# A conv_preact kernel streaming 96 tiles through ten slots: a new place for four of every six loads in SyncE's order

## The chip, the cores and the metric

The kernel runs on one core of one Trainium2 chip. The metric is the device time of one execution in microseconds (us), as the median of several executions. Engines are named as in the profile: PE (TensorE), ACT (ScalarE), DVE (VectorE), POOL (GpSimd), SP (SyncE). SP does no arithmetic here: it issues all transfers between the chip's memory (HBM) and SBUF, on one queue that is carried out by 16 DMA engines.

## The reference

The input is `x` of 16 images, 768 channels, 64 x 64 pixels, in float32, and `offset` of 48 x 2. The output is `x + displace(group_norm(x), offset)`:

```python
def _gn(v, G=32, eps=1e-5):               # 24 channels to a group
    g = v.reshape(B_, G, C_ // G, H_, W_)
    m = jnp.mean(g, axis=(2, 3, 4), keepdims=True)
    s = jnp.var(g, axis=(2, 3, 4), keepdims=True)
    return ((g - m) / jnp.sqrt(s + eps)).reshape(v.shape)
...
    # displace: 48 positions of 16 channels each
    off_px = offset * SCALE
    off_int = lax.stop_gradient(jnp.round(off_px))
    sub = off_px - off_int
...
    shifted = x[:, ch[:, None, None], iyc[:, :, None], ixc[:, None, :]]
    shifted = shifted * mask[None]        # zero where the source lies outside
...
    kern = jnp.exp(-(kx * kx + ky * ky) / (2.0 * SIGMA * SIGMA))
    kern = kern / kern.sum(axis=(1, 2), keepdims=True)
    out = lax.conv_general_dilated(shifted, kern_c[:, None, :, :], window_strides=(1, 1), padding='SAME', feature_group_count=C, ...)
```

So each channel is normalised with the mean and variance of its group, shifted by a whole number of pixels (0, 16, 32 or 48 in each direction, about), smoothed with a 3 x 3 kernel that is a product of a column and a row, and added to `x`.

## The kernel before

The array is cut into 96 tiles of 128 partitions (16 channels by 8 images) and 4096 pixels, which is 2 MB each. Three tiles that share whole groups make a unit, and there are 32 units. SBUF holds ten slots of one tile each, and tile `n` lives in slot `n % 10`: SP loads it there, DVE adds the smoothed part in place, and SP stores it from there. So a load of tile `m` waits until the store of tile `m - 10` has landed (`stored`), and a store of tile `n` waits until DVE has done tile `n` (`tile_done`, which also counts one step of the setup, hence the `+ 2`).

The work on a unit `u` runs across the engines like this:

- PE adds up all pixels of the unit's three tiles in `sums` (L277 in the profile, 8 matmuls a tile, two records each) and waits at each tile for its load (`loaded`). ACT squeezes the result (L440), PE spreads the means to the channels (L287 to L289), and ACT copies them (L445).
- ACT squares each tile around its mean (L455), PE adds the squares up in `variances` (L329 to L337), ACT makes the variance of it (L463), and POOL works out the column weights (L241 to L254).
- ACT copies the source window of each tile, less the mean, into `frame` (L396, L406). DVE makes two passes over it for the rows (L654, L659) and three for the columns, which add into the slot (L663, L666, L669). The first of the three waits for POOL's weights.

PE's order is fixed by hand: it does the sums of unit `u + 1` around the variances of unit `u`. For an odd `u` all three tiles of `u + 1` come ahead of `variances(u)`, for an even `u` two of them do. So the weights of an odd unit wait behind the load of the last tile of the next unit.

SP's order is fixed by hand too. Ten loads come first. Then the stores run in the order of the tiles, and a table with six entries says which loads stand behind each store. Six tiles (two units) are called a pair here. For a pair that begins at tile `b`, load `i` (0 to 5) is that of tile `b + 10 + i`, and it takes the slot of tile `b + i`. In the text a load is called L and a store S with its tile (L34, S24), which is not to be mixed up with a line (L196). An instruction on SP that waits holds up everything behind it on SP. All transfers are 2 MB and go through the same queue. SP's lines are L191 (load) and L196 (store).

Of the kernel before, what the change touches and what calls it, by code (L numbers as in the profile page):

```python
# [5 lines left out]
def build(nc, x, offset, out):  # L6
# [44 lines left out]
    def of_tile(tiles, n):  # L51
        block, half = ORDER[n // UT]
        return tiles[block * UT + n % UT, half]
# [9 lines left out]
    with ctx:  # L63
# [106 lines left out]
        def slot_px(n, a=0, b=PIX):  # L170
            s = n % SLOTS
            return xs[:, s * PIX + a:s * PIX + b]
# [11 lines left out]
        @block.sync  # L184
        def _(sp):
            sp.dma_start(given[:, :, :], offset.partition_broadcast(P)).then_inc(offset_loaded, 16)

            def load(n):
                if n >= SLOTS:
                    sp.wait_ge(stored[n % SLOTS], 16 * (n // SLOTS))  # L190
                sp.dma_start(slot_px(n), of_tile(x_tiles, n)).then_inc(loaded[n % SLOTS], 16)  # L191

            def store(n):

                sp.wait_ge(tile_done, n + 2)
                sp.dma_start(of_tile(out_tiles, n), slot_px(n)).then_inc(stored[n % SLOTS], 16)  # L196

            for n in range(SLOTS):
                load(n)

            AGAIN = [(), (0, 1), (), (2,), (3,), (4, 5)]
            for n in range(TILES):
                store(n)
                for i in AGAIN[n % len(AGAIN)]:
                    m = n - n % len(AGAIN) + i + SLOTS
                    if m < TILES:
                        load(m)
            for s in range(SLOTS):  # L210
                sp.wait_ge(stored[s], 16 * len(range(s, TILES, SLOTS)))
# [507 lines left out]
```

## Time and profile before

| | |
|---|---|
| median of 3 runs | 1015.58 us (1015.21 to 1016.88) |
| the profiled execution, its own time | 1013.46 us |
| its span in the profile | 1011.4 us |
| busy: DVE, PE, ACT, POOL | 82%, 79%, 65%, 39% |
| DMA traffic | 403.10 MB, mean 399 GB/s |
| granted TensorE clock, mean | 0.891 |

The span is the time between the first and the last instruction of the profile, and 2.1 us of the execution's own time lie outside it. Busy shares are means over the whole span. The granted clock is a share of 2.4 GHz.

### The profile page before, as it was taken

How to read it: one execution, taken by the hardware profiler on the slowest of the kernel's cores; microseconds unless marked ns; L12 is line 12 of the kernel's file. 1: busy time of each engine (PE TensorE's matmuls, PEld its weight loads, DVE VectorE, ACT ScalarE, POOL GpSimd, SP SyncE). 2: the span in 40 equal slices, each digit the busy share in tenths (PEclk: the TensorE clock that was granted, in tenths of full speed). 3: DMA queues.
4: the chain of work that ended last, by engine and by line, in shares of the span. 5: the costliest groups of instructions: out<-in, count | busy, mean ns of one | idle time of the engine just before them, and what ended most of it. 6: DMA issues, size and time to landing. Idle time of an engine off the chain costs nothing.

```text
span 1011.4 us, 9224 instructions
## 1 busy us (share of the span) xinstructions
PE 800.2 (79%) x2146; PEld 391.3 (39%) x2146; DVE 828.3 (82%) x550; ACT 657.8 (65%) x555; POOL 394.2 (39%) x348
## 2 busy tenths in 40 slices
PE   1999896988987889696997988888787898978710
PEld 0544343434533435343443533434243443434310
DVE  7588989979879895997969796877959879676796
ACT  7477756567776758576676763746755667783771
POOL 0404547356443401836343262503427336231302
PEclk9999997898889898797999899899898988889955
DMA  8987999999999999999999999999999999999967
GB/s 366 429 360 292 427 425 413 365 411 402 400 412 403 397 413 409 424 415 418 404 408 420 416 428 411 422 416 418 416 391 424 411 415 399 399 402 387 412 259 301
DMA packets 27822, 403.10 MB, mean 399 GB/s; under 512 B 3216, under 2 KB 3216, under 8 KB 3216
## 3 DMA queue, kind: packets, MB, share of 16 engines
q1 hardware_dynamic: 27792, 402.71, 97.0%
q8 instruction: 17, 0.28, 0.1%
q14 instruction: 13, 0.11, 0.0%
HBM read 201.38 MB, written 201.33 MB: 398 GB/s over the span
## 4 chain that ended last, share of the span: by engine, by line
DMA 44%; DVE 22%; PE 12%; ACT 7%; POOL 6%; issue 4%; ACTq 2%; DVEq 2%; SPq 1%; POOLq 0%
DMA out_dram<-xs 36%; PE sum_ps L277 10%; DMA xs<-x_dram 8%; DVE xs L663 5%; ACT frame L396 5%; DVE xs L666 5%; DVE smooth L659 4%; DVE xs L669 4%; DVE smooth L654 4%; POOL small L245 2%; POOL small L248 2%; POOL small L241 2%; ACT unused L455 1%; ACTq L374 1%; DVEq L658 1%
## 5 line engine op out<-in xcount | busy, mean ns | idle before, releaser
L277 PE MATMUL sum_ps<-xs,bands 128*128 128x512 f32 x992 | 499.3, 662 | 31.0 <-DMA xs<-x_dram 31.0
L455 ACT ACTIVATE unused<-xs,small 128x4096 bf16 (+1 forms) x94 | 348.7, 3709 | 16.7 <-ACT small L445 7.1
L396 ACT ACTIVATE frame<-xs,small (+1 forms) x96 | 223.3, 2326 | 176.9 <-DVE smooth L659 174.3
L277 PEld LDWEIGHTS sum_ps<-xs,bands 128*128 128x128 f32 x992 | 207.3, 214 | 285.9 <-issue 260.1
L241 POOL TENSOR_TENSOR small<-small 128x3 f32<-128x3 f32 x32 | 39.4, 1232 | 576.9 <-ACT small L463 576.9
L654 DVE SCALAR_TENSOR_TENSOR smooth<-frame,xs 128x1700 f32 (+5 forms) x96 | 163.5, 1703 | 91.3 <-ACT frame L406 71.7
L277 PE MATMUL sum_ps<-xs,halves 128*128 128x512 f32 x496 | 221.1, 599 | 20.9 <-DMA xs<-x_dram 20.9
L663 DVE SCALAR_TENSOR_TENSOR xs<-smooth,small,xs 128x1700 f32 (+5 forms) x96 | 163.6, 1704 | 60.8 <-POOL small L254 58.5
L659 DVE SCALAR_TENSOR_TENSOR smooth<-frame,xs,smooth 128x1700 f32<-128x1700 f32 (+5 forms) x96 | 163.6, 1704 | 10.4 <-DVE smooth L654 7.3
L669 DVE SCALAR_TENSOR_TENSOR xs<-smooth,small,xs 128x594 f32 (+9 forms) x96 | 159.7, 1664 | 3.4
L666 DVE SCALAR_TENSOR_TENSOR xs<-smooth,small,xs 128x594 f32 (+9 forms) x96 | 159.7, 1664 | 3.4
L277 PEld LDWEIGHTS sum_ps<-xs,halves 128*128 128x128 f32 x496 | 93.6, 191 | 144.8 <-issue 111.8
L248 POOL TENSOR_SCALAR small<-small 128x1 f32<-128x1 f32 x96 | 122.4, 1275 | 8.4
L254 POOL TENSOR_SCALAR small<-base_w,small 128x3 f32<-128x3 f32 x96 | 119.5, 1245 | 9.5
L245 POOL TENSOR_SCALAR small<-small 128x1 f32<-128x1 f32 x96 | 112.1, 1167 | 3.3
L287 PE MATMUL mean_ps<-small,halves 128*128 128x1 f32 x62 | 14.9, 309 | 91.7 <-ACT sum_ps L440 91.7
L463 ACT ACTIVATE small<-var_ps,small 128x3 f32<-128x3 f32 x32 | 8.2, 255 | 79.6 <-PE var_ps L337 77.2
L287 PEld LDWEIGHTS mean_ps<-small,halves 128*128 128x128 f32 x62 | 12.2, 247 | 106.2 <-ACT sum_ps L440 106.2
L406 ACT ACTIVATE frame<-small 128x64 f32 x96 | 31.4, 327 | 12.5 <-ACT frame L396 0.6
L445 ACT ACTIVATE small<-mean_ps 128x3 f32<-128x3 f32 x31 | 5.4, 175 | 38.2 <-PE mean_ps L289 38.2
L440 ACT ACTIVATE sum_ps<-sum_ps 128x512 f32<-128x512 f32 x31 | 19.1, 617 | 9.2 <-PE sum_ps L277 9.2
L329 PEld LDWEIGHTS var_ps<-small,bands 128*128 128x128 f32 x62 | 11.9, 194 | 18.8 <-issue 18.8
(128 smaller groups left out, 280.5 us busy)
## 6 DMA issues: line engine op xcount, KB each, us to landing
xs<-x_dram SPq DMA_DIRECT2D x96, 2048.0 KB, 11.0
out_dram<-xs SPq DMA_DIRECT2D x96, 2048.0 KB, 15.4
smooth<-offset_dram SPq DMA_DIRECT2D x1, 48.0 KB, 4.1
```

Source lines behind the costliest of these rows:

```text
L241: V.tensor_tensor(rstd0, var, power, ALU.pow).then_inc(rstd_step, 1)
L245: V.tensor_scalar(fix[:, column], var[:, column], rstd0[:, column], rstd0[:, column], ALU.mult, ALU.mult).then_inc(rstd_step, 1)
L248: V.tensor_scalar(rstd[:, column], fix[:, column], -0.5, 1.5, ALU.mult, ALU.add).then_inc(rstd_step, 1)
L254: V.tensor_scalar(col_w[:, now * UT + i, :], base_w[:, position, :], rstd0[:, column], rstd[:, column], ALU.mult, ALU.mult).then_inc(col_w ...
L277: last = nc.tensor.matmul(sum_ps[:, :], (FIRST, SAME, SECOND)[i], slot_px(n, c * BANK, (c + 1) * BANK), start=(i == 0 and c == 0), stop=(i ...
L396: nc.scalar.activation(frame[:, bass.ds(b, rows * PITCH)].rearrange("p (r c) -> p r c", c=PITCH)[:, :, LEFT:LEFT + W], xs[:, bass.ds(a, ro ...
L455: nc.scalar.activation(unused[:, :], xs[:, bass.ds(n % SLOTS * PIX, PIX)], ACT.Square, bias=neg_mean[:, i:i + 1], accum_out=squares[:, i:i ...
L654: V.scalar_tensor_tensor(sm, frame_window(-1), side_w[:, bass.ds(n, 1), 0], frame_window(0), ALU.mult, ALU.add).wait_op(tile_done, done_co ...
L659: V.scalar_tensor_tensor(sm, frame_window(1), side_w[:, bass.ds(n, 1), 1], sm, ALU.mult, ALU.add).wait_op(half_smooth, done_count, "sem-ge ...
L663: V.scalar_tensor_tensor(x_window(0, rows), sm, col_flat[:, bass.ds(weights + 1, 1)], x_window(0, rows), ALU.mult, ALU.add).wait_op(smooth ...
L666: V.scalar_tensor_tensor(x_window(1, rows), sm[:, 0:rows - 1], col_flat[:, bass.ds(weights, 1)], x_window(1, rows), ALU.mult, ALU.add).wai ...
L669: V.scalar_tensor_tensor(x_window(0, rows - 1), sm[:, 1:rows], col_flat[:, bass.ds(weights + 2, 1)], x_window(0, rows - 1), ALU.mult, ALU. ...
```

## The change

The table of loads behind stores is replaced. Nothing else differs, and the number of loads, stores and waits is the same.

```diff
-            AGAIN = [(), (0, 1), (), (2,), (3,), (4, 5)]
+            AGAIN = [(), (0,), (), (1,), (2,), (3, 4, 5)]
             for n in range(TILES):
                 store(n)
                 for i in AGAIN[n % len(AGAIN)]:
```

Load 0 stays behind the second store of the pair. Load 1 moves from there to behind the fourth store, load 2 from behind the fourth to behind the fifth, load 3 from behind the fifth to behind the sixth. Loads 4 and 5 stay behind the sixth store. In the last pair but one, load 1 (tile 95) is the last load of all.

On SP, before, a pair in the steady part of the program stands like this. The first row are loads 4 and 5 of the pair ahead, the last are loads 4 and 5 of this pair:

```order
L191 DMA xs<-x_dram 128x4096 x2
L196 DMA out_dram<-xs 128x4096 x2
L191 DMA xs<-x_dram 128x4096 x2
L196 DMA out_dram<-xs 128x4096 x2
L191 DMA xs<-x_dram 128x4096
L196 DMA out_dram<-xs 128x4096
L191 DMA xs<-x_dram 128x4096
L196 DMA out_dram<-xs 128x4096
L191 DMA xs<-x_dram 128x4096 x2
```

On SP, with the change, the same place of the program (the first row are loads 3, 4 and 5 of the pair ahead, the last those of this pair):

```order
L191 DMA xs<-x_dram 128x4096 x3
L196 DMA out_dram<-xs 128x4096 x2
L191 DMA xs<-x_dram 128x4096
L196 DMA out_dram<-xs 128x4096 x2
L191 DMA xs<-x_dram 128x4096
L196 DMA out_dram<-xs 128x4096
L191 DMA xs<-x_dram 128x4096
L196 DMA out_dram<-xs 128x4096
L191 DMA xs<-x_dram 128x4096 x3
```

Counted in transfers, load 1 moves from the fourth place of the pair's twelve to the sixth, load 2 from the seventh to the eighth, load 3 from the ninth to the tenth. Stores 2 to 5 each move one place ahead. Load 0, loads 4 and 5 and stores 0 and 1 keep their places. No other engine's order changes.

## Rows read from the trace of the kernel before

**Rows 1.** The page: the queue's share of the span, and the chain that ended last.

```profile
q1 hardware_dynamic: 27792, 402.71, 97.0%
DMA 44%; DVE 22%; PE 12%; ACT 7%; POOL 6%; issue 4%; ACTq 2%; DVEq 2%; SPq 1%; POOLq 0%
```

**Rows 2.** The chain in order of time, some DMA pieces: start us, us, what.

```profile
2.09 18.29 DMA xs<-x_dram
...
268.22 14.12 DMA out_dram<-xs
...
355.23 14.54 DMA xs<-x_dram
...
905.18 14.56 DMA xs<-x_dram
```

**Rows 3.** The timeline of SP: start us, us to the last issue's end, issues.

```profile
60.92 6.92 SPq L191 DMA_DIRECT2D xs<-x_dram  x2
82.13 3.62 SPq L196 DMA_DIRECT2D out_dram<-xs  x2
...
318.77 5.27 SPq L191 DMA_DIRECT2D xs<-x_dram  x2
324.08 0.96 SPq L196 DMA_DIRECT2D out_dram<-xs  x2
339.38 0.34 SPq L191 DMA_DIRECT2D xs<-x_dram  x1
339.76 0.45 SPq L196 DMA_DIRECT2D out_dram<-xs  x1
344.24 0.34 SPq L191 DMA_DIRECT2D xs<-x_dram  x1
...
476.56 10.05 SPq L191 DMA_DIRECT2D xs<-x_dram  x2
...
628.23 1.79 SPq L196 DMA_DIRECT2D out_dram<-xs  x2
...
905.18 10.06 SPq L191 DMA_DIRECT2D xs<-x_dram  x2
...
931.49 5.20 SPq L191 DMA_DIRECT2D xs<-x_dram  x2
```

**Rows 4.** L191, loads L34 and L35, then L36 and L37.

```profile
L191 SPq DMA_DIRECT2D xs<-x_dram x2: 340/340/340, 318.8 to 323.7; - x2
DMA to landing us min/median/max: 10.2/10.5/10.8
...
L191 SPq DMA_DIRECT2D xs<-x_dram x2: 340/340/340, 339.4 to 344.2; - x2
DMA to landing us min/median/max: 10.9/13.4/15.8
```

**Rows 5.** The timeline of PE from 581 us: start, us, what, [idle before, releaser].

```profile
581.23 7.11 PE L277 MATMUL sum_ps<-xs,bands 128*128 128x512 f32 x16
...
589.12 0.38 PE L287 MATMUL mean_ps<-small,halves 128*128 128x1 f32 x2 [0.78 <-ACT sum_ps L440]
...
593.09 8.59 PE L277 MATMUL sum_ps<-xs,bands 128*128 128x512 f32 x16 [3.14 <-DMA xs<-x_dram]
...
612.58 8.83 PE L277 MATMUL sum_ps<-xs,bands 128*128 128x512 f32 x16 [2.65 <-DMA xs<-x_dram]
```

**Rows 6.** Waits, first of 268.2 to 369.8 us, then of 629.7 to 795: us, times, longest.

```profile
PE sum_ps L277 <- DMA xs<-x_dram: 6.7, 4, 3.7
...
PE sum_ps L277 <- DMA xs<-x_dram: 19.8, 10, 3.4
```

**Rows 7.** The timeline of PE at the last unit's sums, same columns.

```profile
949.68 7.11 PE L277 MATMUL sum_ps<-xs,bands 128*128 128x512 f32 x16
967.89 0.59 PE L287 MATMUL mean_ps<-small,halves 128*128 128x1 f32 x2 [11.10 <-ACT sum_ps L440]
```

## The prediction

> **What bounds the kernel now.** I read the page first, then the chain of waits, then the order and landing of the transfers. The one queue's packets fill 97.0% of the time of 16 engines, so on the face of it the kernel is bound by transfers and a new order of the same transfers can give nothing. The chain says less: DMA is 44% of it, and DVE, PE, ACT and POOL hold 47% [rows 1]. In order of time the chain is on DMA in a few long stretches (the first from 268.22 us to the end of a piece at 355.23 + 14.54 = 369.8, the last ending at 905.18 + 14.56 = 919.7) and on computing between them [rows 2]. So the two take turns, and only what DMA saves in its own stretches can shorten the kernel.
>
> How long are these? 44% of 1011.4 is 445 us, less the first load's piece of 18.3 us [rows 1, 2], which the change can't touch: 427 us.
>
> **Busy is not full speed.** A load is issued the moment its slot's store has landed, so its time to landing tells how fast the queue moved. Where two transfers were ahead of it, three had to pass, and 14.54 and 14.56 us for three [rows 2] make 4.85 us for one. Where one transfer was ahead it should take 9.7 us. It takes more. L34 is issued at 318.77 with only S25 ahead: 10.2. L35 comes at 323.7 with only L34 ahead: 10.8, of which 0.5 is L34's own delay, so 0.6. L36, at 339.38 with S27 ahead, takes 10.9, so 1.2 over, and S28 is issued 0.38 us behind it. L37 has L36 and S28 ahead: 15.8, which is 14.55 and L36's 1.2, so it adds nothing [rows 3, 4]. The loads with two ahead that the chain shows add nothing either [rows 2]. For a whole pair: from 476.56 to 905.18 are seven pairs in 428.62 us, 61.2 each, where twelve transfers at 4.85 are 58.2 [rows 3]. The 3.0 us between are lost while the engines count as busy, and the four loads with one ahead (loads 0, 1, 2 and 5) are where I can see them go.
>
> **The change, part by part.** Nothing is added or removed on any engine. What changes is how much is in the queue when a load is issued. Walking through the new order with stores that are ready when their turn comes:
>
> - Load 0 is issued when store 0 lands, with store 1 alone ahead, as before. Stores 2 and 3 are now issued right behind it, so it looks more like L36 (1.2) than like L34 (0.5), whose successor came 4.9 us later. I take 0.8 and keep 0.5 and 1.2 as bounds.
> - Load 1 waits for store 1, which has long been ahead of load 0: load 0, stores 2 and 3 are in the queue, three ahead. Load 2 has three ahead (store 3, load 1, store 4), load 3 four, load 4 three, load 5 two (loads 3 and 4). By L37's row each of these is free.
>
> So the pair loses 0.8 us where it lost 3.0, and saves 2.2 (1.8 to 2.5). DMA-led stretches are 427 / 61.2 = 7.0 pairs: 15.4 us.
>
> Not all of that arrives. In the first stretch, 101.6 us long, PE idled for loads 6.7 us in four waits. From 629.7 to 795 it idled 19.8 us in ten [rows 6]. Per 100 us that is 6.6 against 12.0, so computing stands close behind DMA in the first stretch and takes over there sooner. Of its 101.6 / 61.2 x 2.2 = 3.7 us I count a third, which takes off 2.4. In the computing stretches I count nothing.
>
> **What the move costs.** Load 1 lands two transfers later, 9.7 us, and it is the last tile of a unit, for which PE waits. Take L59: PE began its sums at 581.23, and as L59's place lies right behind L58's, issued with one ahead 4.9 us after it, like L34 and L35, I place its landing near 578. The sums would start at 587.8 instead, 6.5 us later. Behind them, PE now idles 0.78 us for ACT, 3.14 for L60 and 2.65 for L62 [rows 5], and L60 and L61 come one transfer later too. PE would be through with L61 at about 614.5 and begin L62, which keeps its place in the queue, some 2 us behind the present 612.58. It has taken 8.6 to 8.8 us over a tile after such an idle time and 7.1 in a row of work [rows 5], so it ends L62's sums about where it does now. Behind these are the weights of tile 57 and S57. S57 is issued at about 628.23 + 1.79 - 0.34 = 629.7 [rows 3]. Its new turn comes five transfers after L62's landing (near 612.5), at 636.8, so 7 us of cover are left before the queue runs dry, where 12 were. I cost this at nothing. If the cover is gone, S57 and load 1 of that pair, now behind it on SP, are late by what exceeds it.
>
> At the start, L11 was issued at 60.92 + 6.92 - 0.34 = 67.5, and then SP had nothing to issue until S2 at 82.13. Now L11 stands behind S3, which comes at 82.13 + 3.62 - 0.33 = 85.4 [rows 3], 18 us later. Computing is the bound there until 268 us, and the later loads meet PE with some backlog, so I cost it at nothing, and at up to 2 us as a bound. At the end, L95 is issued behind S87 instead of S85, 9.7 us later than at its present 936.3. PE began its sums at 949.68, and then waited 11.10 us for ACT [rows 7]. L95's landing would move to about 957 less what was saved by then, and the sums would end by 964 even without it, ahead of 967.9. Nothing.
>
> **Sum.** 15.4 - 2.4 = 13.0 us faster. The profiled execution took 1013.46 us of its own, so 1000.5. The median of the runs lies 2.1 above it: 1002.5.
>
> **The rivals.**
>
> A: computing takes over almost at once. DVE is busy 82% of the span, and each stretch of the chain hands over to it. Then each DMA stretch gives perhaps half a microsecond a pair before DVE, ACT and PE are the bound: 3 to 6 us faster, 1011. For it: load 1's lateness falls on PE just when it has least to do, and in the first stretch PE idles little. Against it: PE idles for loads about 12 us in 100 from 629.7 on [rows 6], which is 7 in a pair, three times what the pair would save.
>
> B, slower: the excess doesn't come from the depth of the queue, and stays. Then nothing is saved and only the lateness is left. L59's case shows the price: PE 2 us late on L62, and where it isn't made up by faster matmuls, up to 0.5 us of it reaches each of seven pairs after the cover: 3.5 us slower, 1019. It decides once a pair saves less than 0.5 us. Against it: L36 and L37 are 5 us apart, both with a store ahead, and only the one with one transfer ahead is slow [rows 4].
>
> The Trainium skill speaks for B: DMA: Bandwidth & Descriptors, Anatomy of one DMA, gives a transfer a fixed part of about 2 us besides its bytes at 436 GB/s, and its rules for kernel authors say that this part overlaps when a transfer is issued early. One transfer of 4.8 us ahead would cover 2 us, so a second ahead would buy nothing, and the 3.0 us a pair would be something else, with the time of B. The trace disagrees as far as it goes, with 10.2 to 10.9 us for loads with one ahead where 9.7 would do.
>
> C: more arrives, all of 2.5 us a pair, the first stretch too, and computing stretches shorten as PE finds its tiles loaded: 17 us or more, 998 or below. Against it: DVE and PE have 18 and 21% of the span idle, so far more than that would have to come out of their own chain.
>
> D: no change, where A's small gain meets B's lateness.
>
> **How the numbers follow.** My forecast (8 to 17 us faster) has 0.60, A 0.14, C 0.10, D 0.05 and B 0.11. The range runs from 993 (C with its whole 3.0 us a pair, and 2 us from computing stretches) to 1012.5 (A's lower end), and leaves out B, D and little of C. The likeliest case's own range is 998.5 to 1007.5. A measurement of this kernel can tell about 0.2%, 2 us, from no change. Faster by more holds the forecast, A's most part and C: 0.83. Same: 0.06. Slower: 0.11.
>
> **What the profile after should show.** A pair in DMA-led stretches near 59 us where it was 61.2. Loads 1 to 5 issued with two or more ahead, with landing times of 14.5 us and up in whole multiples of 4.85, and load 0 alone at 10.2 to 10.9. DMA's share of the chain falls, that of DVE and PE grows. Store 3 of each pair (S57 is one) is issued at DVE's pace, with the queue nearly empty at times in computing stretches. I am wrong if loads with three ahead still lose a microsecond, if load 1's lateness shows as PE idle before the last sums of even pairs and then in DVE's wait for weights, or if the granted clock falls as PE idles less.

## The result and the profile after

The changed kernel takes 1010.85 us (median of 20 runs) against 1016.74 us (20 runs of the kernel before, the three shown above among them). The ratio is 0.9948, with a 95% interval of 0.993 to 0.9965: 0.5% faster, some 5 us, where 13 us were forecast. The direction was right and 1010.85 lies in the stated range of 993 to 1012.5, but the size of the gain was not right. The profiled execution has a span of 1008.2 us, where it was 1011.4.

The page of the changed kernel: the queue's line, and the chain that ended last. Behind it stands the same last line of the kernel before.

```profile
q1 hardware_dynamic: 27792, 402.71, 96.2%
DMA 30%; PE 23%; DVE 23%; ACT 8%; POOL 6%; issue 5%; ACTq 2%; DVEq 2%; SPq 0%; POOLq 0%
DMA xs<-x_dram 27%; PE sum_ps L276 20%; DVE xs L662 5%; DVE xs L665 5%; ACT frame L395 5%; DVE smooth L658 5%; DVE xs L668 4%; DVE smooth L653 4%; DMA out_dram<-xs 4%; POOL small L240 2%; POOL small L244 2%; POOL small L247 1%; ACTq L373 1%; ACT unused L454 1%; DVEq L657 1%
```

```profile
DMA out_dram<-xs 36%; PE sum_ps L277 10%; DMA xs<-x_dram 8%; DVE xs L663 5%; ACT frame L396 5%; DVE xs L666 5%; DVE smooth L659 4%; DVE xs L669 4%; DVE smooth L654 4%; POOL small L245 2%; POOL small L248 2%; POOL small L241 2%; ACT unused L455 1%; ACTq L374 1%; DVEq L658 1%
```

Against [rows 1], DMA's share of the chain has fallen from 44 to 30%, and PE's has grown from 12 to 23%. All line numbers behind the table are smaller by one. Most of what DMA gave up, PE has taken, and the lines by name say where: before, stores held 36% of the chain and loads 8%. Now loads hold 27%, stores 4%, and PE's sums 20% where they held 10%. The chain runs through loads and the PE that waits for them.

The timeline of SP in the changed kernel (start us, us to the last issue's end, issues), one pair in the second half and the place that the prediction counted from and to:

```profile
473.58 10.05 SPq L191 DMA_DIRECT2D xs<-x_dram  x2
...
623.02 0.34 SPq L191 DMA_DIRECT2D xs<-x_dram  x1
623.41 7.62 SPq L196 DMA_DIRECT2D out_dram<-xs  x2
631.07 0.98 SPq L191 DMA_DIRECT2D xs<-x_dram  x1
637.69 0.33 SPq L196 DMA_DIRECT2D out_dram<-xs  x1
639.06 0.34 SPq L191 DMA_DIRECT2D xs<-x_dram  x1
...
894.74 10.05 SPq L191 DMA_DIRECT2D xs<-x_dram  x2
```

The same seven pairs as in [rows 3] take 894.74 - 473.58 = 421.16 us, 60.2 each. It was 61.2, and 59 were forecast. In the pair shown, S56 and S57 are issued 7 us apart (623.41, and 623.41 + 7.62 - 0.34 = 630.7), since S57 waits for DVE, and L65 (load 1) comes right behind.

The landing of three groups of loads in the changed kernel, load 0 (L64), loads 1 and 2 (L65, L66) and loads 3 to 5:

```profile
L191 SPq DMA_DIRECT2D xs<-x_dram x1: 340/340/340, 623.0 to 623.0; - x1
DMA to landing us min/median/max: 11.1/11.1/11.1
...
L191 SPq DMA_DIRECT2D xs<-x_dram x2: 340/662/985, 631.1 to 639.1; - x2
DMA to landing us min/median/max: 17.6/18.5/19.4
...
L191 SPq DMA_DIRECT2D xs<-x_dram x3: 328/340/340, 643.9 to 663.4; - x3
DMA to landing us min/median/max: 14.6/19.4/24.3
```

Loads 2 to 5 behave as forecast: 14.6 is three transfers, 19.4 four, 24.3 five, nothing over. Load 0, with one ahead, takes 11.1 where 9.7 would do, so it loses 1.4 us here, more than the 0.8 that was taken and than the upper bound of 1.2. This pair is kind to load 1. Over all pairs (what each landing in the trace comes later than 4.85 us behind the one before it) load 0 loses 1.2 us on average and load 1 0.6: between 1.0 and 1.8 in each of the first seven pairs, nothing in the last eight. In the kernel before, loads 0, 1, 2 and 5 lost 0.2, 0.8, 0.9 and 1.1.

The waits of the whole span, first in the kernel before, then in the changed one (us, times, longest):

```profile
DVE smooth L654 <- ACT frame L406: 71.7, 37, 5.1
...
PE sum_ps L277 <- DMA xs<-x_dram: 51.9, 26, 3.7
...
ACT sum_ps L440 <- PE sum_ps L277: 9.2, 1, 9.2
```

```profile
PE sum_ps L276 <- DMA xs<-x_dram: 102.4, 34, 6.9
DVE smooth L653 <- ACT frame L405: 91.5, 43, 7.4
...
ACT sum_ps L439 <- PE sum_ps L276: 50.4, 12, 9.2
```

PE idles 102.4 us for loads, where it was 51.9. Tile by tile, 72.3 us of it are for load 1, for which PE never idled before, and 24.3 for load 3. ACT waits for PE's sums 50.4 us in 12 waits, where it was one wait at the start. DVE waits 20 us more for ACT's frame. Take L29. In the kernel before, this is PE at its sums and at the means behind them (start, us, what, [idle before, releaser]):

```profile
277.86 7.11 PE L277 MATMUL sum_ps<-xs,bands 128*128 128x512 f32 x16
289.45 0.59 PE L287 MATMUL mean_ps<-small,halves 128*128 128x1 f32 x2 [4.48 <-ACT sum_ps L440]
```

and in the changed kernel

```profile
284.99 9.29 PE L276 MATMUL sum_ps<-xs,bands 128*128 128x512 f32 x16 [6.00 <-DMA xs<-x_dram]
295.06 0.38 PE L286 MATMUL mean_ps<-small,halves 128*128 128x1 f32 x2 [0.78 <-ACT sum_ps L439]
```

Before, PE didn't wait for L29 and idled 4.48 us ahead of the means, 3.7 more than the 0.78 that remain now. Now it idles 6.00 us for L29, runs the sums at 9.29 us instead of 7.11, and the means come 5.6 us later. The landing of L29, first in the kernel before, then in the changed one:

```profile
L191 SPq DMA_DIRECT2D xs<-x_dram x1: 340/340/340, 261.9 to 261.9; - x1
DMA to landing us min/median/max: 10.7/10.7/10.7
```

```profile
L191 SPq DMA_DIRECT2D xs<-x_dram x1: 1970/1970/1970, 270.2 to 270.2; - x1
DMA to landing us min/median/max: 14.7/14.7/14.7
```

It landed at 261.9 + 10.7 = 272.6 and now does at 270.2 + 14.7 = 284.9, 12.3 us later and not 9.7. Its store (S21) does wait for DVE, but the queue didn't run dry there: S20 was under way until 273.6. The trace shows the other 2.6 us as L28, ahead of it, landing 1.7 us later than before, and L29 losing 0.9 us more in the queue than it did. And DVE is late in turn. ACT squeezes the sums between the frames of tiles 25 and 26, so its wait of 4.2 us for PE puts off the frame of tile 26. DVE's first pass over it, before and after, with DVE's wait for the frame:

```profile
303.54 3.55 DVE L654 SCALAR_TENSOR_TENSOR smooth<-frame,xs 128x3200 f32 x1 [1.36 <-ACT frame L406]
```

```profile
308.52 3.55 DVE L653 SCALAR_TENSOR_TENSOR smooth<-frame,xs 128x3200 f32 x1 [5.04 <-ACT frame L405]
```

The last pass of tile 27 on DVE, before and after:

```profile
324.07 0.54 DVE L669 SCALAR_TENSOR_TENSOR xs<-smooth,small,xs 128x306 f32 x1
```

```profile
329.06 0.54 DVE L668 SCALAR_TENSOR_TENSOR xs<-smooth,small,xs 128x306 f32 x1
```

So by tile 27 DVE is 5.0 us behind the kernel before. Of these, 3.7 are this wait. The rest it had from the start: it was 0.3 us behind at tile 8 and 1.5 at tile 11, whose own load (L11) landed 22.8 us later than before.

The issues and landings of all 192 transfers show where the span goes. With no loss and no gap, each of the 191 behind the first would land 4.85 us after the one before it, 926.4 us in all. The first landing and the end take 11 to 12 us. What comes on top, in us:

| | before | changed | loads 2 and 3 moved alone (e2 below) |
|---|---|---|---|
| lost with transfers in the queue | 53.3 | 41.0 | 31.3 |
| queue empty, and starting again | 20.5 | 29.5 | 26.3 |
| span | 1011.4 | 1008.2 | 996.1 |

The change took 12.3 us of loss out of the queue and put 9.0 us of emptiness in.

### The profile page after: what moved, and what is told of

Its sections match the earlier page's. It is cut to its first block, busy times and chain, and to the rows that moved or that the text cites. A ratio compares the mean times of both kernels' runs of the same rounds, so it can differ in the third digit from the quotient of the medians.

```text
span 1008.2 us, 9224 instructions
## 1 busy us (share of the span) xinstructions
PE 798.7 (79%) x2146; PEld 387.5 (38%) x2146; DVE 828.5 (82%) x550; ACT 659.2 (65%) x555; POOL 400.2 (40%) x348
## 3 DMA queue, kind: packets, MB, share of 16 engines
q1 hardware_dynamic: 27792, 402.71, 96.2%
## 4 chain that ended last, share of the span: by engine, by line
DMA 30%; PE 23%; DVE 23%; ACT 8%; POOL 6%; issue 5%; ACTq 2%; DVEq 2%; SPq 0%; POOLq 0%
DMA xs<-x_dram 27%; PE sum_ps L276 20%; DVE xs L662 5%; DVE xs L665 5%; ACT frame L395 5%; DVE smooth L658 5%; DVE xs L668 4%; DVE smooth L653 4%; DMA out_dram<-xs 4%; POOL small L240 2%; POOL small L244 2%; POOL small L247 1%; ACTq L373 1%; ACT unused L454 1%; DVEq L657 1%
## 5 line engine op out<-in xcount | busy, mean ns | idle before, releaser
L240 POOL TENSOR_TENSOR small<-small 128x3 f32<-128x3 f32 x32 | 45.9, 1434 | 567.8 <-ACT small L462 567.8
L276 PE MATMUL sum_ps<-xs,halves 128*128 128x512 f32 x496 | 228.5, 615 | 29.2 <-DMA xs<-x_dram 29.1
L653 DVE SCALAR_TENSOR_TENSOR smooth<-frame,xs 128x1700 f32 (+5 forms) x96 | 163.6, 1704 | 103.2 <-ACT frame L405 91.5
L662 DVE SCALAR_TENSOR_TENSOR xs<-smooth,small,xs 128x1700 f32 (+5 forms) x96 | 163.6, 1704 | 44.4 <-POOL small L253 42.2
L439 ACT ACTIVATE sum_ps<-sum_ps 128x512 f32<-128x512 f32 x31 | 18.4, 593 | 50.4 <-PE sum_ps L276 50.4
L286 PE MATMUL mean_ps<-small,halves 128*128 128x1 f32 x62 | 12.8, 276 | 34.3 <-ACT sum_ps L439 34.3
L405 ACT ACTIVATE frame<-small 128x64 f32 x96 | 31.5, 328 | 12.1
L286 PEld LDWEIGHTS mean_ps<-small,halves 128*128 128x128 f32 x62 | 10.1, 206 | 48.8 <-ACT sum_ps L439 48.8
L335 PE MATMUL var_ps<-small,bands 128*128 128x1 f32 x62 | 12.0, 262 | 13.8 <-ACT unused L454 13.8
(128 smaller groups left out, 272.6 us busy)
```

The lines of the kernel that those rows point to most:

```text
L240: V.tensor_tensor(rstd0, var, power, ALU.pow).then_inc(rstd_step, 1)
L276: last = nc.tensor.matmul(sum_ps[:, :], (FIRST, SAME, SECOND)[i], slot_px(n, c * BANK, (c + 1) * BANK), start=(i == 0 and c == 0), stop=(i ...
L653: V.scalar_tensor_tensor(sm, frame_window(-1), side_w[:, bass.ds(n, 1), 0], frame_window(0), ALU.mult, ALU.add).wait_op(tile_done, done_co ...
L662: V.scalar_tensor_tensor(x_window(0, rows), sm, col_flat[:, bass.ds(weights + 1, 1)], x_window(0, rows), ALU.mult, ALU.add).wait_op(smooth ...
```

## The experiments

All change only what their diff shows. Those that ran on one chip beside the same runs of the kernel before are: e1 to e4; t1 to t3 with c1; e5 to e7 with t4; e8 to e11; e12; e14. The kernel before had medians of 1012.8 to 1020.0 us in these groups, so across them the ratios to it are what compares, and times only roughly.

**Without computing.** Three orders, with every engine but SP left out. The output is `x` as loaded.

```diff
-                sp.wait_ge(tile_done, n + 2)
+                sp.wait_ge(loaded[n % SLOTS], 16 * (n // SLOTS + 1))
...
-        @block.gpsimd
...
```

t1_transfers_before, the order before. Expected:

> All computing is left out (PE, ACT, DVE and POOL do nothing, the output is x as loaded), and a store waits for its load instead of for DVE. The order of the transfers is that of the kernel before. Depth theory (a load issued with one transfer ahead loses about 1 us, with two or more nothing): 192 transfers at 4.85 us are 931, and 3.0 us in each of 15 pairs are 45: 975 to 985 us, with a pair taking about 61 us. If the excess comes from computing beside the transfers, the pair takes 58.2 and the kernel 937 to 945.

Measured: 987.4 us, span 985.2. That is 2 us above what was expected.

t2_transfers_after, the changed order. Expected:

> The same without computing, with the order of the changed kernel. Depth theory: only load 0 of a pair has one ahead, 0.8 to 1.2 us a pair, so 945 to 955 us, some 30 us under the same with the order before. If the excess stays with the turn from a store to a load, both orders have four such turns a pair, and this takes as long as the other, 975 to 985.

Measured: 963.1 us, span 960.3. It missed the expectation by 8 us.

t3_transfers_loads23, the order of e2 below. Expected:

> The same without computing, with loads 2 and 3 moved and load 1 in its old place: loads 0 and 1 have one ahead. Depth theory: 1.2 to 2.0 us a pair, 955 to 965 us, between the two others.

Measured: 956.4 us, span 953.7. In the range, but the fastest of the three and not between the others.

A load in t1 and a load in t2 that both stand behind a store with one transfer ahead (L52 here and there; load 0 of its pair):

```profile
L191 SPq DMA_DIRECT2D xs<-x_dram x1: 340/340/340, 493.5 to 493.5; - x1
DMA to landing us min/median/max: 9.7/9.7/9.7
```

```profile
L191 SPq DMA_DIRECT2D xs<-x_dram x1: 340/340/340, 477.8 to 477.8; - x1
DMA to landing us min/median/max: 10.8/10.8/10.8
```

That the order of the same bytes is worth 24 us (31 for t3), with no engine computing, shows that the loss hangs on the order of the transfers and not on computing beside them: rival B's premise is out. The busy share hides all of it: 99.5, 99.9 and 100.0% in t1, t2 and t3. But the same two rows show what the forecast missed. Load 0 loses nothing when load 1 follows it 4.85 us later, as before, and 1.1 us when two stores follow at once (0.1 and 1.1 on average over the 15 pairs). So the change saves 24.3 / 15 pairs = 1.6 us a pair even without computing, not 2.2. t3, where load 1 still follows load 0, saves 2.1.

**Which of the moves gives what.** e4_change_again, the changed kernel beside the others, expected:

> The changed kernel as it is, on the same chip as the three others, to compare them with. All theories: 4 to 7 us faster than before.

Measured: 1013.23 us, ratio 0.9954 (0.993 to 0.9977).

e1_load1_only:

```diff
-            AGAIN = [(), (0,), (), (1,), (2,), (3, 4, 5)]
+            AGAIN = [(), (0,), (), (1, 2), (3,), (4, 5)]
```

> Load 1 alone moves by two places; loads 2 and 3 keep theirs, and load 5 again has one transfer ahead of it. Theory 1 (what the deeper queue gives is taken back by load 1 landing two transfers later, for which PE and then ACT wait): the pair still loses some 1 us at load 5 and 1 us at load 0 and has all of load 1's lateness, so 1 to 4 us faster than before and slower than the whole change. Theory 2 (computing is the bound for any order, about 5 us under the kernel before): 4 to 6 us faster, as the whole change.

Measured: 1015.62 us, ratio 0.9968 (0.9938 to 0.9997). Barely faster than before.

e2_loads23_only:

```diff
-            AGAIN = [(), (0,), (), (1,), (2,), (3, 4, 5)]
+            AGAIN = [(), (0, 1), (), (), (2,), (3, 4, 5)]
```

> Loads 2 and 3 move by one place each, load 1 stays behind load 0. Loads 2 and 5 get two or more ahead, loads 0 and 1 keep one. Theory 1 (load 1's lateness takes the gain back): 1.8 us a pair saved at loads 2 and 5, no lateness of load 1, ACT's wait for PE's sums as small as before (about 10 us in all): 8 to 10 us faster than before, so faster than the whole change. Theory 2 (computing is the bound for any order): 5 us faster, same as the whole change. Theory 3 (loads 2 and 3, one transfer later, are what PE waits for): 0 to 3 us faster.

Measured: 999.57 us, ratio 0.9819 (0.9787 to 0.9852). That is 17 us faster than before, nearly twice what the expectation's highest theory gave, and 13.7 us faster than the changed kernel on the same chip. Repeated as e7_loads23_again, expected:

> Loads 2 and 3 moved alone, once more, on the same chip as the two others: 998 to 1002 us.

Measured: 1000.69 us, ratio 0.9854 (0.9816 to 0.9893). And as e11_loads23_third, expected:

> Loads 2 and 3 moved alone, on the same chip as the three others, to compare them with: 998 to 1002 us.

Measured: 999.25 us, ratio 0.9829 (0.9802 to 0.9857). So two of the three moves give the whole gain and more, and moving load 1 costs most of it again. The waits of e2, the same lines as above:

```profile
PE sum_ps L276 <- DMA xs<-x_dram: 25.8, 15, 6.5
...
ACT sum_ps L439 <- PE sum_ps L276: 9.2, 1, 9.2
```

ACT's wait for PE is gone but for its one wait at the start (9.2 us, as in the kernel before), and PE idles for loads a quarter as long as in the changed kernel.

e3_load1_one_place:

```diff
-            AGAIN = [(), (0,), (), (1,), (2,), (3, 4, 5)]
+            AGAIN = [(), (0,), (1,), (2,), (), (3, 4, 5)]
```

> Load 1 stands behind store 2 in place of store 3, one transfer later than before instead of two; load 2 stays behind store 3; loads 3, 4 and 5 behind store 5. All but load 0 have two or more ahead. Theory 1 (load 1's lateness takes the gain back): half the lateness with all of the depth, 9 to 12 us faster than before. Theory 2 (computing is the bound for any order): 5 us faster. Theory 3 (loads 2 and 3 are what PE waits for): as load 2 is back in its place, 5 to 8 us faster.

Measured: 1008.97 us, ratio 0.9915 (0.9883 to 0.9948). Between the two, nearer to the changed kernel.

**Is computing the bound for any order?** e2 has answered it with no for an order that gives 5 us. c1_short_transfers asks how far down it would go:

```diff
+                part = PIX if n < SLOTS else PIX // 4
-                sp.dma_start(slot_px(n), of_tile(x_tiles, n)).then_inc(loaded[n % SLOTS], 16)
+                sp.dma_start(slot_px(n, 0, part), of_tile(x_tiles, n)[:, 0:part]).then_inc(loaded[n % SLOTS], 16)
...
-                sp.dma_start(of_tile(out_tiles, n), slot_px(n)).then_inc(stored[n % SLOTS], 16)
+                sp.dma_start(of_tile(out_tiles, n)[:, 0:PIX // 4], slot_px(n, 0, PIX // 4)).then_inc(stored[n % SLOTS], 16)
```

> The changed kernel with transfers of a quarter: after the first ten loads every load and store moves 1024 of a tile's 4096 pixels, so most of the output is not written and the computing runs on old pixels; its instructions are all there. It tells how long computing takes when transfers hardly count. Theory 2 (computing is the bound for any order): 990 to 1005 us, close to the changed kernel. Theory 1 (load 1's late landing is what holds PE up): clearly less, 940 to 975 us, with PE's idle time on loads and ACT's on PE's sums near nothing.

Measured: 971.2 us, span 969.5. With short transfers, computing in this order of the engines takes 971 us, and transfers alone 956 to 963. The changed kernel's 1011 lies 40 us above the greater of the two, so it is bound by how they wait for each other and not by either alone.

**Load 0's loss or load 1's lateness?** Against e2 the changed kernel differs in two ways. e5_wait_before_store2 tried to take the first away:

```diff
             for n in range(TILES):
+                if n % len(AGAIN) == 2:
+                    sp.wait_ge(stored[(n - 1) % SLOTS], 16 * ((n - 1) // SLOTS + 1))
                 store(n)
```

> The changed kernel, and SP waits before store 2 of each pair until store 1 has landed, so that load 0 is no longer followed at once by stores 2 and 3. Load 1 stays two places late. Depth theory with what was seen so far: load 0's loss falls from 1.2 us to some 0.2 us. If that loss is what took the gain, this is 10 us or more faster than the changed kernel; if load 1's lateness took it, this is within 4 us of the changed kernel, 1006 to 1014 us, with ACT's wait for PE's sums still about 50 us in all.

Measured: 1013.34 us, ratio 0.9976 (0.994 to 1.0012). t4_transfers_wait is the same without computing:

> Without computing (the output is x as loaded, a store waits for its load): the changed order with the wait for store 1 before store 2. If load 0's loss comes from stores issued right behind it while one transfer is ahead: 0.2 us a pair in place of 1.1, so 945 to 953 us where the same without the wait took 963. If it comes from the one transfer ahead alone: 960 to 966.

Measured: 976.3 us, 13 us slower than t2 without the wait. Both expectations on the queue missed. Loads 0 and 1 of a pair in t4 (L52 and L53), from issue to landing:

```profile
L191 SPq DMA_DIRECT2D xs<-x_dram x2: 339/658/977, 484.4 to 490.0; - x2
DMA to landing us min/median/max: 10.6/15.6/20.5
```

L52 still loses 0.9 us over the 9.7 of two transfers, though the next issue, here a store, comes 4.8 us later. L53, issued at 490.0, has L52 (landing at 484.4 + 10.6 = 495.0) and two stores ahead, so it should land at 495.0 + 3 x 4.85 = 509.5, and lands at 490.0 + 20.5 = 510.5, another microsecond late, with three ahead. So spacing the issues is no cure, three transfers ahead don't always save a load from the loss, and e5 decides nothing between the two causes.

e8_pe_waits_two puts lateness onto PE alone, on top of e2:

```diff
                     pe.wait_ge(loaded[n % SLOTS], 16 * (n // SLOTS + 1))
+                    if n >= SLOTS and (n - SLOTS) % 6 == 1:
+                        s = n - SLOTS - 1 + 3
+                        pe.wait_ge(stored[s % SLOTS], 16 * (s // SLOTS + 1))
```

> Loads 2 and 3 moved alone (the fast order), transfers left as they are, and PE starts its sums of load 1's tile only when store 3, two transfers behind it in that order, has landed. It puts the lateness of load 1 alone onto PE, without any of load 0's greater loss. If lateness is what took the gain: 8 to 13 us slower than the same without the wait (999.6 and 1000.7 us so far), so 1008 to 1014, with ACT waiting some 50 us for PE's sums. If the queue's loss at load 0 took it: 999 to 1003 us.

Measured: 999.33 us, ratio 0.9832 (0.9805 to 0.9859), against 999.25 without the wait. Lateness was expected to cost 8 to 13 us: PE and ACT wait more, as they were meant to (ACT 34.8 us and not 50), and it costs nothing.

```profile
PE sum_ps L279 <- DMA out_dram<-xs: 50.0, 14, 6.7
...
ACT sum_ps L442 <- PE sum_ps L279: 34.8, 9, 9.2
```

e9_pe_waits_one is the same with `+ 2`:

> The same with store 2, one transfer behind load 1. If lateness is what took the gain: 1 to 5 us slower than without the wait, 1001 to 1005, as the first 5 us or so lie under PE's own backlog and ACT's order. If the queue's loss took it: 999 to 1002 us.

Measured: 999.8 us, ratio 0.9817 (0.979 to 0.9844). Nothing, as for two. e12_pe_waits_three is the same with `+ 4`:

> Loads 2 and 3 moved alone, transfers unchanged, and PE starts its sums of load 1's tile only when store 4, three transfers behind load 1 in that order, has landed, some 15 us after the load. With two transfers (9.9 us behind the landing) nothing was lost. In the changed kernel load 1 lands 11 to 12.5 us later than before, since it also stands behind store 3's wait for DVE. If there is an edge close above 10 us: 5 us or more slower than without the wait, 1005 to 1018. If PE's lateness costs nothing here at all: 999 to 1003.

Measured: 1007.28 us, ratio 0.9868 (0.9836 to 0.9899). By the ratio this is 4 us slower than e11, by the medians 8. The kernel of e2 did not run on this chip, and the interval of the ratio overlaps those of its three sessions, so the size is rough. But all six runs (1005.5 to 1010.0) lie above all 17 of e2's kernel (997.4 to 1002.6). ACT's wait for PE goes beyond that of the changed kernel (50.4), PE's idle time is about the same:

```profile
PE sum_ps L279 <- DMA out_dram<-xs: 98.0, 15, 9.4
...
ACT sum_ps L442 <- PE sum_ps L279: 72.4, 14, 10.1
```

DVE waits 99.5 us for ACT's frame here, 73.9 in e2 and 91.5 in the changed kernel. So lateness begins to cost somewhere between 10 and 15 us. Against the kernel before, load 1 of the changed kernel lands 22.8, 16.1, 13.6 and 12.3 us later in the first four pairs, and 11.0 on average over all 15.

e14_extra_transfer puts a loss into the queue alone, on top of e2 (e13, with a tensor in SBUF for it, gave no result, since SBUF had no room; here it goes from HBM to HBM):

```diff
                     if m < TILES:
                         load(m)
+                        if i == 0:
+                            if n >= 6:
+                                sp.wait_ge(extra_loaded, 16 * (n // 6))
+                            sp.dma_start(extra[:, :], of_tile(x_tiles, m)[:, 0:640]).then_inc(extra_loaded, 16)
```

> Loads 2 and 3 moved alone, and an extra transfer of 640 of a tile's 4096 columns (0.33 MB, 0.76 us at the full rate), from the input to a spare tensor in HBM, right behind load 0 of each pair; nothing reads it. It adds to the queue about what the changed order loses there more than this one (0.85 us a pair), without moving a load. If the queue's loss took the gain: 8 to 13 us slower than without it, 1007 to 1013. If computing leads for most of the time: 0 to 5 us slower, 999 to 1005.

Measured: 1007.47 us, ratio 0.9928 (0.99 to 0.9956), 0.8 to 1.1% slower than e2 in its three sessions. The waits tell this case from lateness:

```profile
PE sum_ps L282 <- DMA xs<-x_dram: 35.5, 16, 7.4
...
ACT sum_ps L445 <- PE sum_ps L282: 9.2, 1, 9.2
```

ACT doesn't wait for PE beyond its wait at the start, yet 8 us are gone. In the trace loads 0 and 1 of a pair land 6.5 us apart, where it was 5.6 in e2. That is 13 us in 15 pairs, of which some 8 reach the end, though DMA is 22% of the chain in e2.

**Other loads' places.** e6_all_one_late:

```diff
-            AGAIN = [(), (0,), (), (1,), (2,), (3, 4, 5)]
+            AGAIN = [(), (), (0, 1), (), (2,), (3, 4, 5)]
```

> Loads 0 and 1 both stand behind store 2, load 2 behind store 4, loads 3 to 5 behind store 5: every load of a pair has two or more ahead, and loads 0 to 3 are one transfer later than before. If only the queue's losses counted it would be the fastest of all, 990 to 997 us. If a load's place counts as much (loads 0 and 1 now wait for DVE's third tile of the pair, which is often late), it gives most of that back: 1005 to 1018 us.

Measured: 1019.78 us, ratio 1.0037 (1.0012 to 1.0063), slower than before, with a queue that is never shallow by the table. In its trace load 1 loses 1.2 us on average even so, and the queue stands empty for 29.5 us, where it was 13.8 in the kernel before (the time to start again not counted). e10_loads2345_last:

```diff
-            AGAIN = [(), (0, 1), (), (), (2,), (3, 4, 5)]
+            AGAIN = [(), (0, 1), (), (), (), (2, 3, 4, 5)]
```

> Load 2 goes one store further too: loads 0 and 1 behind store 1, loads 2 to 5 behind store 5. The queue is as deep or deeper, load 2 lands one more transfer later. If lateness of any load that PE waits for costs: 1003 to 1010 us. If only load 1's place matters: 998 to 1002 us.

Measured: 1010.18 us, ratio 0.9917 (0.9879 to 0.9954). One store further for load 2 takes half of e2's gain. The waits of SP in it (us, times, longest), then in e2:

```profile
SPq L196 <- DVE xs L668: 617.3, 84, 35.6
SPq L191 <- DMA out_dram<-xs: 298.1, 62, 15.3
```

```profile
SPq L191 <- DMA out_dram<-xs: 484.0, 82, 16.6
SPq L196 <- DVE xs L668: 422.5, 73, 35.7
```

With the load behind one more store, SP waits more for DVE and less for slots. The changed kernel has the same mark (in the kernel before it was 218.3 us for DVE and 700.2 for slots):

```profile
SPq L196 <- DVE xs L668: 506.7, 79, 35.6
SPq L191 <- DMA out_dram<-xs: 400.8, 51, 18.2
```

## Why the prediction was half right

**That order alone can free time in a queue that counts as 97% busy** was right. t1 and t2 show it with no engine computing, and loads 2 to 5 lose nothing in the pair shown of the profile after. The fall of DMA's share in the chain and the slow stores at store 3 came as described.

**The saving of 2.2 us a pair** was the first wrong size. The term is load 0's loss, "I take 0.8 and keep 0.5 and 1.2 as bounds". It measured 1.1 in t2 and 1.4 in the pair shown of the profile after, while in the order before load 0 loses least of the four (0.5 at L34, 0.0 in t1's row, 0.2 on average). Without computing the saving is 1.6 us a pair over all pairs. In the kernel it was 1.1 (61.2 to 60.2) over the seven pairs counted. Seven pairs at 1.1 make 7.5 us, where the term was 15.4. Load 1 wasn't free either, as "by L37's row" had it: L29, issued at 270.2 with S20 and S21 ahead, lands 14.7 us later, and S20 landed 3.3 us after L29's issue, so with two transfers of 4.85 behind that it should have taken 13.0, and it lost 1.7. In the first seven pairs it is always so (1.0 to 1.8 us). The prediction counted "with stores that are ready when their turn comes"; here S21 was issued with S20 alone in the queue.

**"What the move costs ... I cost this at nothing"** is the other step that failed, and the greater one: without the move of load 1 the same kernel is 13.7 us faster. It had three faults. It left the queue out: load 1 was costed as late and not as a load that makes the queue lose, but t3, where it keeps its place, is 6.7 us faster than t2 with no engine computing. It placed load 1 9.7 us later by counting transfers, and measured are 11.0 on average and 12.3 to 22.8 in the first four pairs. And it was checked at one tile (L59) and at the two ends. At L29, where the chain of the kernel before has just gone from computing to DMA (268.22), it costs DVE 3.7 us. The start cost 1.2 us by tile 11, inside its bound of 2. What the step may have right is the cover: in e8, 10 us of lateness is free, so at the 9.7 us of the estimate it might have been. The signs that the prediction named for being wrong came in part: loads with three ahead lost a microsecond (L53 in t4), and PE idles for load 1. But DVE's wait for the weights fell (58.5 to 42.2 us), and its wait for ACT's frame grew (71.7 to 91.5).

**How much each cause took.** e2 is 13.7 us faster than the changed kernel on one chip. The greater loss in the queue put in alone costs about 8 us (e14), lateness of some 15 us put in alone 4 to 8 (e12), of 10 us nothing (e8). Both are shown as causes that can act. In the table above, the profiled runs of the two lie 12.1 us apart, with 9.7 us more lost in the queue and 3.2 more of empty queue, so the loss seems the greater part. But that is an account and no proof of cause: no run has the changed kernel's lateness without its loss in the queue, and e5, meant to be that run, missed. The shares stay open.

**The rivals.** A (computing takes over, 3 to 6 us faster, 1011) gave the time that was measured, for a reason that doesn't hold: computing is no bound at 1011, since e2 does the same computing at 1000 and c1 at 971. It was not DVE's own speed but DVE, PE and SP waiting for each other through load 1. B's premise fell with t1 and t2. That one transfer ahead would cover the fixed part of a transfer, which the prediction held for B, was its own step, and in t1 loads with one ahead lose 0.1, 0.6, 0.8 and 1.3 us on average (loads 0, 1, 2 and 5). C's 17 us came, but in e2's order, and D is outside the interval, which begins at 3.6 us faster. The 0.60 on the forecast was too much for a sum in which one term was costed at nothing after one look at one tile.

## What to carry to other kernels

When transfers of loads and stores share a queue and each load waits for its slot's store, place the load so that at least two transfers are ahead of it when its wait ends, which mostly helped here, and read time to landing in multiples of one transfer: the busy share doesn't show the loss. Move first the loads that the other engines reach last, and leave in place the one for which a chain of engines waits; here two of three moves gave 17 us and the third took nearly 14 of them back. Before costing a move at nothing, follow the moved instruction behind every wait it newly stands behind (here a store that waits for DVE) and on to the engine that ends the chain (here from load 1 to PE's sums, ACT's frame and DVE), at several places, above all where the lead goes from computing to transfers.

## What the runs showed of the hardware

A DMA queue can lose time with all 16 engines counted as busy. In the kernels without computing, 402.71 MB take spans of 985.2, 960.3, 953.7 and 975.4 us in four orders, at busy shares of 99.5, 99.9, 100.0 and 99.3%. With one 2 MB transfer ahead, L52 takes 9.7 us to land if a load is issued 4.9 us behind it (t1), 10.8 if two stores are issued behind it at once (t2), and 10.6 if one store is issued 4.8 us behind it (t4). With two or more ahead most loads of the rows shown land in whole multiples of 4.85 us, but L53 in t4 and L29 in the changed kernel lose 1.0 and 1.7 us with three and two ahead. Over all pairs, the loads that lose more than 0.3 us on average are loads 1, 2 and 5 in t1 (0.6, 0.8, 1.3), load 0 in t2 (1.1), load 1 in t3 (0.6), and loads 0 and 1 in t4 (1.0, 1.1). So the depth at the issue tells most of the loss and not all. Why the queue loses the time is not settled by these runs.
